# Context tiles split before they are turned, and turned by DMA instead of TensorE

## The reference

```python
# x, ctx_1024: (8, 512, 512) f32;  8 heads of 64;  8 experts, 2 chosen for each token
x = x + tanh(g_xattn[0]) * attention(layernorm(x), ctx_1024, Wq, Wk, Wv, Wo, bo)
#   q = ln(x) @ Wq;  k, v = ctx @ Wk, ctx @ Wv;  softmax(q k^T / 8) @ v;  @ Wo + bo
x = x + tanh(g_ffn[0]) * experts(layernorm(x), gate_w, Wu, Wv, Wo)
#   logits = x @ gate_w;  top 2;  softmax of the two;  (silu(x Wu_e) * (x Wv_e)) @ Wo_e, weighted
```

## Time and profile before

| | |
|---|---|
| median of 3 runs | 1000.81 us (999.84 to 1004.14) |
| profiled execution, its time | 1002.09 us |
| its span | 1000.4 us |
| busy: PE, PEld | 88 %, 54 % |
| busy: DVE, ACT, POOL | 70 %, 57 %, 53 % |
| attention steps (32) | from about 52 us to 712 us |
| expert stage | from about 785 us to the end |

### The profile page before, as it was taken

One profiled execution on the slowest core, in us unless ns is written; L12 is line 12 of the kernel. 1 busy time (PEld: TensorE's weight loads), 2 busy tenths in 40 slices (PEclk: granted clock), 3 DMA queues, 4 the chain that ended last, 5 costly groups with the idle time before them and its releaser, 6 DMA issues. The chain is left out here.

```text
span 1000.4 us, 22929 instructions
## 1 busy us (share of the span) xinstructions
PE 881.5 (88%) x8250; PEld 536.4 (54%) x8250; DVE 695.5 (70%) x1661; ACT 568.0 (57%) x1022; POOL 528.5 (53%) x643
## 2 busy tenths in 40 slices
PE   4877999999999899999989999998782899899990
PEld 2334555555555555555555555554441788677770
DVE  5568897677877877787787778768668655454540
ACT  4367676556756655766565576555630466455550
POOL 6212244353457546546745644556756254766765
PEclk9999999999999999999999999999995899999995
DMA  7537942844544364354436333664255598999997
GB/s 266 145 96 231 314 123 74 241 118 115 155 121 113 87 192 111 79 148 132 105 91 190 110 78 75 200 208 117 90 175 203 139 193 190 186 218 205 218 175 100
DMA packets 120511, 153.22 MB, mean 153 GB/s; under 512 B 42961, under 2 KB 75729, under 8 KB 119633
## 3 DMA queue, kind: packets, MB, share of 16 engines
q1 hardware_dynamic: 96624, 101.77, 35.8%
q0 software_dynamic: 16864, 37.40, 18.9%
q10 hardware_dynamic: 6912, 12.59, 4.0%
HBM read 67.06 MB, written 56.56 MB: 124 GB/s over the span
## 5 line engine op out<-in xcount | busy, mean ns | idle before, releaser
L708 POOL TENSOR_TENSOR Pl<-P,Ph 128x512 f16<-128x512 f32 x128 | 152.5, 1203 | 167.0 <-ACT Ph L796 166.7
L793 ACT ACTIVATE P<-ST 128x512 f32<-128x512 f32 x256 | 154.4, 603 | 112.7 <-PE ST L1516 109.1
L994 DVE TENSOR_REDUCE mx<-MX 128x1 f32<-128x512 f32 x256 | 168.6, 684 | 26.1 <-PE MX L1501 25.8
L796 ACT ACTIVATE Ph<-ST 128x512 f16<-128x512 f32 x256 | 155.8, 609 | 0.4
L758 POOL DMA_INDIRECT out_dram<-V,Ph x78 | 121.9, 1562 | 64.0 <-ACT V L948 42.3
L1718 PE MATMUL MX<-heads,tiles 128*128 128x256 f16 x936 | 116.8, 276 | 7.6 <-DVE heads L1397 7.6
L1528 PE MATMUL PV<-V,Ph 128*128 128x65 f16 x1024 | 111.0, 194 | 7.9 <-issue 7.5
L1528 PEld LDWEIGHTS PV<-V,Ph 128*128 128x128 f16 x1024 | 96.1, 97 | 28.3 <-issue 9.6
L1530 PE MATMUL PV<-V,Ph 128*128 128x64 f16 x1024 | 111.2, 195 | 0.0
L1532 PE MATMUL PV<-V,Pl 128*128 128x65 f16 x1024 | 110.8, 193 | 0.0
L1718 PEld LDWEIGHTS MX<-heads,tiles 128*128 x936 | 90.3, 99 | 27.9 <-issue 10.9
(11 more groups left out here) (268 smaller groups left out, 1888.7 us busy)
## 6 DMA issues: line engine op xcount, KB each, us to landing
heads<-expert_rows SPq DMA_DIRECT2D x39, 516.0 KB, 4.9
heads<-q_hi SPq DMA_DIRECT2D x124, 64.0 KB, 2.6
heads<-k_hi SPq DMA_DIRECT2D x124, 64.0 KB, 2.7
second_norm<-in_x_dram SPq DMA_DIRECT2D x28, 256.0 KB, 3.1
out_dram<-second_norm SPq DMA_DIRECT2D x28, 256.0 KB, 2.6
tiles<-in_x_dram ACTq DMA_DIRECT2D x24, 256.0 KB, 3.1
tiles<-in_ctx_dram ACTq DMA_DIRECT2D x24, 256.0 KB, 3.8
expert_rows<-zero_rows SPq DMA_DIRECT2D x8, 516.0 KB, 5.4
```

The costliest lines, as they stand in the source:

```text
L708: nc.gpsimd.tensor_tensor(Pl[:, hh, c, :], P32[:, c, :], Ph[:, hh, c, :], ALU.subtract).then_inc(pl_pool, 1)
L793: nc.scalar.activation(P32[:, c, :], ST[:, c % 2, :], ACT.Exp, scale=0.125 / SC2).then_inc(p_ready, 1)
L796: nc.scalar.activation(Ph[:, hh, c, :], ST[:, c % 2, :], ACT.Exp, scale=0.125 / SC2).then_inc(ph_ready, 1)
L994: nc.vector.tensor_reduce(out=mx[:, k // TT, k % TT:k % TT + 1], in_=MX[:, (k + odd) % 2, :], axis=AXX, op=ALU.max).then_inc(mx_taken, 1)
```

## The change

- Context tiles of the batches after the first are no longer transposed on TensorE. ScalarE writes the hi part in the natural layout from the loaded tile (`context_hi`) into `c_split`, which shares its memory with the x tile that has just been normalised; VectorE writes the lo part (`context_lo`); SyncE's queue turns both by DMA transposes into `cT` (`turn_context`, two DMAs a tile, 56 in all). The k projection of j = 2 waits for `ctx_turned`, and so does `load_tile`, on ScalarE.
- `ranks` are made in the step j = 2 behind the logits, in a general bank. MX holds only score tiles and `oT`, and the waits for the other two are gone.
- Residuals from the third on are loaded by ScalarE's queue, in the middle of the step before.

```diff
+        if j == 2 and b >= 2:
+            names.append(("ranks", b - 2))
...
-        if kind == "ranks" and 4 * n + 9 < steps - 4:
-            places[kind, n] = "MX", (4 * n + 9) % 2, ("oT", 4 * n + 5)
-        elif kind == "oT" and g < steps:
+        if kind == "oT" and g < steps:
             places[kind, n] = "MX", g % 2, g
-        elif kind == "c" and n >= TT and n % 2 == 0:
-            places[kind, n] = "MX", 1 - g % 2, g
...
+        c_split = slab(0, 2).rearrange("p (t a d) -> p t a d", t=TT, a=2)
...
+            def turn_context(n):
+                b, t = divmod(n, TT)
+                if b >= 2:
+                    sp.wait_ge(filled, use["k", 4 * b - 7] + 1)
+                sp.wait_ge(ctx_lo, n - TT + 1)
+                for a in range(2):
+                    sp.dma_start_transpose(cT[b % 2][a][:, :, t * P:(t + 1) * P], c_split[:, t, a]).then_inc(ctx_turned, 16)
...
-                    load_residual(g - 4)
+                    if g < 6:
+                        load_residual(g - 4)
...
                 if g >= 5:
                     turn(g - 5)
+                if b < B - 1 and j < 2:
+                    turn_context(4 * (b + 1) + 2 * j)
                 if b:
                     store_x2(g - 4)
+                if b < B - 1 and j < 2:
+                    turn_context(4 * (b + 1) + 2 * j + 1)
...
+            def context_hi(n):
+                t = n % TT
+                act.wait_ge(xn_ready, n + 1)
+                act.wait_ge(c_ld[t], (n // TT + 1) * 16)
+                nc.scalar.activation(c_split[:, t, 0], c_in[:, t, :], ACT.Copy, scale=XS).then_inc(ctx_hi, 1)
...
             def load_tile(b, t):
+                act.wait_ge(ctx_turned, (b - 1) * TT * 2 * 16)
...
+            def load_residual(n):
+                k = n % 2
+                act.wait_ge(x2_st[k], n // 2 * 16)
+                act.wait_ge(xn2_ready, 2 * (n - 1))
+                nc.scalar.dma_start(X2[:, k, :], xt[n // TT, n % TT]).then_inc(x2_ld[k], 16)
...
                 if 5 <= g < STEPS - 1:
                     normalise2(g - 5)
+                if more and j < 2:
+                    context_hi(ahead)
...
                 exps(hd + 1, 1, 1)
+                if 5 <= g < STEPS - 1:
+                    load_residual(g - 3)
                 if b:
                     hi_part(("oT", g - 4), oT[0][:], 1.0)
                 if more:
                     side(ahead)
+                    if j < 2:
+                        context_hi(ahead + 1)
...
+            def context_lo(n):
+                t = n % TT
+                dve.wait_ge(ctx_hi, n - TT + 1)
+                nc.vector.scalar_tensor_tensor(out=c_split[:, t, 1], in0=c_in[:, t, :], scalar=XS, in1=c_split[:, t, 0],
+                                               op0=ALU.mult, op1=ALU.subtract).then_inc(ctx_lo, 1)
...
+                if more and j < 2:
+                    context_lo(ahead)
                 if b:
                     lo_part(("oT", g - 4), oT[1][:], oT[0][:], 1.0)
...
                     side(ahead)
+                    if j < 2:
+                        context_lo(ahead + 1)
...
             def token_tile(n):
                 pe.wait_ge(xn_ready, n + 1)
                 transposes(("x", n), xn[:, n % 2, :])
-                pe.wait_ge(c_ld[n % TT], (n // TT + 1) * 16)
-                transposes(("c", n), c_in[:, n % TT, :])
...
-                            pe.wait_ge(evacuated, use["x" if n == "q" else "c", TT * (b + 2) - 1] + 1)
+                        if j == 2 and n == "q":
+                            pe.wait_ge(evacuated, use["x", TT * (b + 2) - 1] + 1)
+                        if j == 2 and n == "k":
+                            pe.wait_ge(ctx_turned, (b + 1) * TT * 2 * 16)
```

More of the change, by code:

```diff
@@ L68, in side @@
             return [], []
-        return tuple([("x", t), ("c", t)] if j < 2 else [("v", t)] for t in tiles)
+        return tuple([("x", t)] if j < 2 else [("v", t)] for t in tiles)
     for g in range(steps):
@@ L82, in bank_uses @@
             names.append(("out", g - 4))
-        if j == 1 and b >= 2:
-            names.append(("ranks", b - 2))
         names += second
@@ L102, in bank_places @@
     for kind, n in uses:
[L103 to L106 removed]
+        g = n + 4
+        if kind == "oT" and g < steps:
             places[kind, n] = "MX", g % 2, g
[L108 to L109 removed]
         else:
@@ L326, in layer @@
         c_ld = [sem(f"ctx_loaded{t}") for t in range(TT)]
+        ctx_hi, ctx_lo = sem("ctx_hi_written"), sem("ctx_lo_written")
+        ctx_turned = sem("ctx_parts_turned")
         ln_ready = sem("ln_factors_ready")
@@ L451, in load_residual @@
             def load_residual(n):
[L452 to L455, removed]
+                sp.dma_start(X2[:, n, :], xt[0, n]).then_inc(x2_ld[n], 16)
             def load_last_residuals():
@@ L880, in side @@
                 def side(n):
-                    turned_hi(n) if j < 2 else v_hi(n)
+                    turned_hi(n, "x") if j < 2 else v_hi(n)
                 loads = j == 2 and b < B - 2
@@ L1308, in side @@
                 def side(n):
-                    turned_lo(n) if j < 2 else v_lo(n)
+                    turned_lo(n, "x") if j < 2 else v_lo(n)
                 maxima(0, 1, 2, 3)
@@ L1327, in step @@
                     take_logits(g - 6)
+                if j == 2 and b >= 2:
+                    take_ranks(b - 2)
                 if nmax:
@@ L1351, in step @@
                 head_out(hd, b % 2)
-                if j == 1 and b >= 2:
-                    take_ranks(b - 2)
                 if b == 0:
@@ L1441, in bank @@
                     return G[:, k, :]
-                if name[0] == "ranks":
-                    pe.wait_ge(evacuated, use[since_] + 1)
-                elif name[0] == "oT":
-                    pe.wait_ge(mx_taken, min(since_ + 2, STEPS) * 2 * TT)
-                else:
-                    pe.wait_ge(mrow_ready, since_ + 2)
+                pe.wait_ge(mx_taken, min(since_ + 2, STEPS) * 2 * TT)
                 return MX[:, k, :]
@@ L1495, in row_max_scores @@
                     since(pe, mx_taken, g * (2 * TT) + k - (1 if k > 1 else 0))
-                b, j = divmod(g - 2, 4)
-                if k == 0 and b >= 1:
-                    pe.wait_ge(evacuated, use[("ranks", b - 2) if j == 1 and 2 <= b < B - 1 else ("oT", g - 6)] + 1)
-                if k == 1 and g >= 2 and b < B - 1 and j < 2:
-                    pe.wait_ge(evacuated, use["c", TT * (b + 1) + 2 * j] + 1)
+                if k == 0 and g >= 6:
+                    pe.wait_ge(evacuated, use["oT", g - 6] + 1)
                 nc.tensor.matmul(MX[:, (k + g) % 2, :], Q1[:, s, h, t * P:(t + 1) * P], K1[:, s, h, :],
@@ L1656, in step @@
                     logits(g - 6)
+                if j == 2 and b >= 2:
+                    ranks(b - 2)
                 scores(b, j, 5)
@@ L1674, in step @@
                 weighted(hd, 3)
-                if j == 1 and b >= 2:
-                    ranks(b - 2)
                 if more:
```

3 lines of the change are left out of this document (1 added, 2 removed).

## The result

| | before | after |
|---|---|---|
| median of 4 runs each, taken side by side | 1000.92 us | 1014.89 us (1013.28 to 1019.96) |
| ratio | | 1.0152 (1.0122 to 1.0182) |
| profiled execution, its time | 1002.09 us | 1013.28 us |
| its span | 1000.4 us | 1011.6 us |
| mean granted TensorE clock | 0.964 | 0.957 |

The changed kernel is 1.5% slower. The forecast was 1004.3 us and no measurable change; the time lies inside the range given, near its upper end, but not in the case held likeliest. The two profiled executions stand 11.2 us apart, the medians 14.0.

A forecast was written before the change was run, and what follows sets the result against it. TensorE's own order was taken as the path, wherever it does not wait. Batches 2 to 6 +2.0, batch 1 -0.5 and the first batch +2.0 gave +3.5: 1005.6 us profiled, 1004.3 on the median, range 992 to 1016.

The forecast's parts named there:

- rival B: SyncE's queue: six turns of a batch's last tile land 2 us late; +12, some 1016 with the first batch; chance 0.24.
- TensorE's saving: 112 context transposes leave TensorE, at most 13.2 us, 24 with waits; time taken ahead of a wait only lengthens it.
- j = 0, no gain: First step of a batch: context_hi ahead of oT_hi costs 0.5, the second context tile's 0.47 goes; sum 0.
- The wait of 1.7 us: TensorE before the output projection, waiting for oT_lo: the 0.70 wait grows to 1.7.
- j = 1 into j = 2, the stretched chain: context_lo, slowed beside GpSimd, delays VectorE's chain; q projection of j = 2 still some 23.6 us after j = 1 starts.
- +0.4 a batch for batches 2 to 6: Ranks' 0.35 now in j = 2, 0.1 less in front: a batch loses 0.4, five batches +2.0.
- the 1.7 us: TensorE enters j = 2 some 1.7 us earlier, but the gain is lost waiting for the last tile's x parts.
- The first batch, +2 (-1 to +4): Two context turns, 5.0 us, delay an expert load on SyncE's queue; 1.9 late, twice, up to 3.8; taken as +2.
- Batch 1, -0.5: No ranks in this batch, so it can only win 0.6 + 0.47 - 0.5; taken as -0.5 (-2 to 0).
- My landing estimate: Last turned context tile lands at 613.0 to 613.9, before the k projection of j = 2 at 614.99; no TensorE wait.
- A: Rival: TensorE bound, the transposes' time comes back; -12 to -24, so 977 to 989; chance 0.14.
- C: Rival: VectorE slips in ahead of GpSimd, no port cost; 996.3, or 1000.5 with late turned tiles; chance 0.20.

The follow-up runs named there:

- e8: Changed kernel with the first context tile's split (context_hi, context_lo) moved behind the split of oT; 1.0142 of the kernel before.
- e1: Changed kernel with the second tile's context_lo moved behind the lo part of the second x tile; 1.0148 of the kernel before.
- the yardstick: The changed kernel unchanged, run again beside the follow-up kernels on their chip; 1.0127 of the kernel before.
- e5: Changed kernel, but context tiles made in the first batch's steps are transposed by TensorE as before; 1.0073 of the kernel before.
- e4: Kernel before with only the moved ranks and the residuals on ScalarE's queue, context tiles still transposed by TensorE; 1.0019 of the kernel before.
- e7: e5 plus context turns ahead of SyncE's other transfers and the second tile's context_lo late in j = 1 only; 1.0051 of the kernel before.

## Why the prediction was wrong

Three terms of the sum failed: the steps of the first batch (+2 forecast, +6.8 measured), batch 1 (-0.5, +4.0) and batches 2 to 6 (+2.0, +6.8). The time still lies in the range, but that is luck: its upper end, 1016, was the price of rival B, turned tiles that are 2 us late in six batches, and that did not happen.

**TensorE's saving is given away ahead of waits: right.** No step is shorter by what was taken off TensorE except the second, and that ends in a wait. 18.07 busy us of 19.83 where it was 19.77 of 21.89.

**j = 0, no gain: right in the sum.** 19.74 became 19.83. The +0.5 of `context_hi` is real: e8 takes 0.52 off. The wait of 1.7 us that I placed in front of the output projection is there in j = 1, but in two pieces: 1.06 for the exponential, ahead of the score tile, and 0.70 for `oT_lo` (1.76 together). In j = 0 there was no wait of 0.70 before, as I had written, but one of 0.25; it became 0.34 and 0.70. Since `context_hi` delays ScalarE's whole run, the first that wait for it pays, and that is the exponential.

**j = 1 into j = 2, the stretched chain: right, to 0.2 us.** q projection 23.39 us after the step's start (forecast 23.6 or later), `context_lo` 1.30 instead of 0.68 beside GpSimd, and e1 moves both. The Trainium skill ("SBUF — State Buffer", section "SBUF: two separate sides") has this as an exclusive lock between VectorE operations with two SBUF inputs and GpSimd ones that read SBUF. The trace agrees: of the 28 instances of `context_lo`, the 16 that start while a GpSimd tensor operation runs take 1225 to 1304 ns; ten with none beside them take 670 to 682; and two, in the first batch, start ahead of GpSimd's operation and take 670, and there it is GpSimd's that takes long, 1729 and 2281 ns instead of its median of 1159.

**+0.4 a batch for batches 2 to 6: right at full clock where the batch looks like batch 6, wrong in the sum.** At 1.00 the second and third step take 19.83 + 25.33 = 45.16 us (the yardstick's batch 6) against 44.90 (batches 4 and 5 before), and with the first step +0.35 a batch; batch 3 of the first pair, at 1.00, costs 0.5. The sum was +6.8 instead of +2.0, for two reasons.

The first is a step that I left out. I wrote that the 1.7 us are "gone" at the q projection, and did not write down the wait that this makes: 1.7 and the 0.52 that already stood there, 2.2 us, priced at its own length only. TensorE's granted clock falls behind it in batches 4 to 6: 26.69 us, against 25.68 in batch 3 of the same execution and 25.33 in the yardstick's batch 6. That is 1.0 to 1.4 us in three batches, 3.0 to 4.1 in all. No wait in the rows that I had read was over 0.79, but the trace held longer ones, and I did not look for what they do. In the last batch of the kernel before, a wait of 1.86 us for the row maxima, and the clock behind it:

```profile
696.36 0.39 PE L1501 MATMUL MX<-heads 128*128 128x512 f16 x1 [1.86 <-DVE mx L994]
```
```profile
696.70:700.20 3.50, 3.29 (x20) 1.55 (x20) 3.39 (x6) 1.09 (x2) 2.40 (x5) 0.51 0.03 12
```

The Trainium skill ("TensorE: Matmul & The Clock Gate", section "The HAM clock gate") says that the clock follows how busy TensorE has lately been, and that how many matmuls of one kernel run at the lower clock differs from run to run. Both are seen here: the wait of 2.28 us is followed by a fall in three steps of five in the first pair's execution, in one of two in the yardstick's, and in none of five in e5's.

The second is batch 2, +2.1 at a clock of 1.00. I counted the waits of 0.79 and 0.52 as gone in five batches; in the kernel before batch 2 has neither, and its second step is 20.90 us, not 21.89, so there was 1.0 less to win. And ScalarE waits 1.93 us for the turned tiles there. How much of the rest that wait costs, no run separates.

**The first batch, +2 (-1 to +4): too small by over three times.** The two steps cost 6.8 us in the first pair, 7.1 between e4 and the yardstick, and e5 takes 5.8 of them off (46.8 to 41.0). I had costed the four transposes at 5.0 us, as the delay of one load. They took 6.54 and 5.33, and they delay everything behind them in the queue, `arrange` and the row maxima too, not the load alone. Then the tiles land late for k in g = 2, which I had checked only for a whole batch. The clock that falls behind the wait of 2.77 us is in the 6.8 too, and in no term of mine.

**Batch 1, -0.5: wrong sign.** +4.0 in the first pair, 1.0 of it in the second step with the clock at 0.92; +2.5 between e4 and the yardstick. My landing estimate, 1 to 2 us ahead of the k projection, was made in batch 6. In batch 1 the same queue also clears blank rows (1.33 us), a pair of turns took 4.27 us instead of 2.5, and the tiles are 1.85 us late. I never asked what else the queue issues in each batch.

**The rivals.** B, SyncE's queue late, was right in kind and wrong in extent: it decides in the first two batches, and in the other five the k projection waits in no step of the first pair and in one of the yardstick (0.46 us, batch 2). My own sign for it was that ScalarE has no wait over 0.5 us for load_tile; it has three, 4.17, 4.22 and 1.93 us, in the third steps of the first three batches. It becomes the next bound as soon as q is mended (e1, e7). A and C did not occur. My chances had 0.24 for B and none for a half of it together with a fall of the clock.

**Ranks and residuals, +0.35 and 0: right** within e4's interval (1.0019, 0.9993 to 1.0044; its third step is 0.3 longer).

What stays open: why single transposes take 1.4 to 3.0 us to issue where most of the 56 take 1.2 to 1.3. The longest is in batch 1, but batches 5 and 6 have one each of 2.27 and 2.09, so it needn't be the load of the first batches; no run separates it. And on the chips of the experiments the last steps of a batch and the expert stage are longer in all kernels; this was not followed up.

## What to carry to other kernels

Before moving work from the busiest engine to a queue, find the batch in which that queue is fullest and cost the move there: everything issued behind it is late by its whole length, and reordering only chooses who waits. Work taken from TensorE ahead of a wait isn't neutral: the longer wait can cost the clock on top, so shorten what it waits for in the same edit. And two consumers with nearly equal slack, as q and k here, are to be mended together, since each mend alone gives its gain to the other's wait: four edits, three of which show nothing by themselves (in the forms tried, 1.0142 to 1.0148), turn +1.3% into -0.4%.

## What the hardware showed

- A DMA transpose of a 128 x 512 tile of f16 holds SyncE's queue for 1.26 us (median of 56), up to 3.0, and lands 2.5 us after its issue (median), up to 6.7.
- Behind a wait of 2.15 to 2.28 us TensorE's granted clock fell in 9 third steps of 24: from 534.40 to 537.70 the windows give 0.52, and the step took 1.0 to 1.4 us more. Behind a wait of 2.45 to 2.52 us it fell in three of five places in one execution (22.94 to 23.18 us against 21.6), and behind two waits of 1.06 and 0.70 close together in three of five in another (21.51 against 19.83) and in none in the first pair's.
- A VectorE operation of 670 ns with both inputs in SBUF takes 1225 to 1304 when it starts while a GpSimd tensor operation runs (16 instances). Where it starts first, it keeps its 670, and GpSimd's operation is the long one (0.73 us instead of 0.23 in e1).
